# Attention and quantized FFN block on eight cores: the sign additions of the weight preparation move ahead of the next tile's scaling on VectorE

## The chip, the cores and the metric

One Trainium2 chip, all 8 NeuronCores. Every core runs the same program on its own data. The metric is the device time in microseconds (us) of the slowest core; lower is better.

## What is computed

Each of 4 sequences has 4096 tokens of width 1024; a core computes the output of one half of a sequence (2048 tokens, 16 tiles of 128), but needs keys and values of all 32 tiles.

```python
q = softmax((x @ Wq.T + bq) @ Wfq.T + bfq)      # x is layer-normed; k likewise with Wk, Wfk
v = x @ Wv.T + bv
scores = einsum('bhsd,bhtd->bhst', q, k)        # 16 heads of 64
ctx = einsum('bhst,bhtd->bhsd', scores / scores.sum(-1), v)
x = x + ctx
# FFN on layernorm(x); every matrix product is "bitlinear":
scale = 1 / mean(abs(w));   wq = clip(round(w * scale), -1, 1) / scale      # weights: -1, 0, +1
scale = 127 / max(abs(x));  xq = clip(round(x * scale), -128, 127) / scale  # activations, per token
x = x + bitlinear(silu(bitlinear(h, w_gate)) * bitlinear(h, w_up), w_down)
```

Since no exponent stands between scores and values, the kernel keeps one matrix (k times v, summed over all tokens) instead of scores.

## The kernel before, in words

The program is written as five lists of instructions, one for each engine, in the order in which the Python code emits them (class `Plan`). The order on an engine is the order of emission; between engines there are semaphores: `dv`, `ac` and `pe` emit for VectorE (DVE), ScalarE (ACT) and TensorE (PE), and each wait names a counter (`cDV`, `cAC`, `cPE`) and the value it must have reached. No scheduler moves anything.

The stages follow one another: the attention weights are combined (to 264 us), the sweep over the 32 token tiles (264 to 1326 us), then the gate and up weights are loaded and the first two FFN products run for 16 tiles (`main_mm`), then the down product. The loads for the FFN stage wait for a fence on all counters at the sweep's end.

The sweep is the loop `for t in range(TKV)` at L588. For a tile t it does:

- L597 (DVE): `xr_buf` = the tile times its reciprocal deviation, from the statistics that the turn before made.
- L604 (PE): eight transposes of `xr_buf` into `pbtr`; L610 (DVE) copies `pbtr` to `xrT`.
- L541 to L552 (PE, in `emit_proj`): the key projection into `pbA`, then the value projection into `pbV`, 16 + 4 matmuls each. L616 (DVE) takes the row maximum, L619 (ACT) the exponent, L627 and L632 (DVE) write the scaled values to `vstage`, L650 (PE) adds k times v into `pbK`.
- `emit_next_tile_stats`: the load of tile t + 1 (issued on SyncE, SP, L573) and its statistics (L329 to L348 on DVE, L352 and L356 on ACT, L360 to L371). For t < 16 the query projection and its exponent and transposes follow (L660 to L679).

Beside that runs the preparation of the three FFN weights, 24 chunks of 128 x 4096 numbers. Tiles 0 to 11 carry the first pass, sums of absolute values (`emit_prep1`, L404). At tile 12 `emit_finalize` makes the three thresholds. Then the second pass: at the end of each of the turns 13 to 24, two chunks get their signs on ACT (`emit_prep2_signs`, L492 and L497: two passes over the chunk, one with the threshold added, one with it subtracted), and the loads of two further chunks are issued from ACT's queue (L479). The sum of the two sign images is the quantized chunk: `emit_prep2_add`, L510 on DVE, which waits for L497 (`cAC`), and the store L516 on SP, which waits for L510. `prep2_drain_adds` emits all additions whose signs have been emitted; before the change it is called at L600, in the turn that follows, between L597 and the transposes of that turn. So the turns 14 to 25 hold two additions each.

SP's list around a turn is: two stores of chunks (L516), then the load of the tile after next (L573).

Of the kernel before, what the change touches and what calls it, by code (L numbers as in the profile page):

```python
# [76 lines left out]
def build_nc(TQ=16, TKV=32, dbg=()):  # L77
# [395 lines left out]
    def emit_prep2_load(k):  # L473
        wi, wdram, sl_, dst_ = prep_chunks[k]
        s = k % 2
        lsem = ("dWP", "dWP1")[s]
        prep2_ld[k] = dma("scalar", lsem,
                          lambda e, wdram=wdram, sl_=sl_, dst_=dst_, s=s:
                          e.dma_start(dst_(pchunk, s), sl_(wdram.ap())),  # L479
                          waits=[("cAC", prep2_ac.get(k - 2)),  # L480
                                 ("cAC", prep1_ac[len(prep_chunks) - 2 + s])])
# [21 lines left out]
    def emit_prep2_add(k):  # L503
        wi, wdram, sl_, dst_ = prep_chunks[k]
        sdram = (s_q["g"], s_q["u"], s_q["d"])[wi]
        s = k % 2
        ssem = ("dWS", "dWS1")[s]
        SGP = ppb[:, s * 4 * D:(s + 1) * 4 * D]
        PWQ = pwq[:, s * 4 * D:(s + 1) * 4 * D]
        vW = dv(lambda e, SGP=SGP, PWQ=PWQ: e.tensor_tensor(  # L510
            PWQ, SGP, PWQ, op=ALU.add),
            waits=[("cAC", prep2_ac[k])], drain=True)
        prep2_dv[k] = vW
        prep2_st[k] = dma("sync", ssem,
                          lambda e, sdram=sdram, sl_=sl_, dst_=dst_, s=s:
                          e.dma_start(sl_(sdram.ap()), dst_(pwq, s)),  # L516
                          waits=[("cDV", vW)])

    def prep2_drain_adds():
        while p2a[0] < p2s[0]:  # L520
            emit_prep2_add(p2a[0])
            p2a[0] += 1
# [65 lines left out]
    for t in range(TKV):  # L588
# [8 lines left out]
        xr_dv[t] = dv(lambda e, xap=xap, t=t, XR=XR: e.tensor_single_scalar(  # L597
            XR, xap, stat[:, STT["r"] + t:STT["r"] + t + 1], op=ALU.mult),
            waits=[(xw_sem, vL), ("cAC", stats_marks[t][1])])
        prep2_drain_adds()  # L600

        vT = None
        for j in range(CH):
# [91 lines left out]
        if fin_done[0]:  # L695
            for _ in range(2):
                if p2l[0] < NP2 and p2l[0] - p2s[0] < 2:
                    emit_prep2_load(p2l[0])
                    p2l[0] += 1

    while prep_i < len(prep_chunks):
        emit_prep1(prep_i)
# [541 lines left out]
```

How the kernel before makes its waits and increments, by code:

```python
                    def body(e):  # L63
                        for fn, waits, inc, inc_by, drain in stream:
                            for sem, val in waits:
                                e.wait_ge(sems[sem], val)
                            if drain:
                                e.drain()
                            inst = fn(e)
                            if inc is not None:
                                inst.then_inc(sems[inc], inc_by)
```

## Time and profile before

| | us |
|---|---|
| median of 2 runs | 2328.51 |
| the two runs | 2325.71, 2331.30 |
| the profiled execution | 2329.61 |
| its span, slowest core (7) | 2328.0 |
| spans of the eight cores | 2305.4 to 2328.0 |
| outside the span | 1.6 |

The profile below is of core 7 unless a group says otherwise. Starts are us from the first instruction; "idle before" is how long the engine had stood still, with what ended it behind the arrow. The granted clock of TensorE is given as a share of 2.4 GHz: 0.5 is the lower of its two levels, 1.2 GHz.

### The profile page before, as it was taken

How to read it: one execution, taken by the hardware profiler on the slowest of the kernel's cores; microseconds unless marked ns; L12 is line 12 of the kernel's file. 1: busy time of each engine (PE TensorE's matmuls, PEld its weight loads, DVE VectorE, ACT ScalarE, POOL GpSimd, SP SyncE). 2: the span in 40 equal slices, each digit the busy share in tenths (PEclk: the TensorE clock that was granted, in tenths of full speed). 3: DMA queues.
4: the chain of work that ended last, by engine and by line, in shares of the span. 5: the costliest groups of instructions: out<-in, count | busy, mean ns of one | idle time of the engine just before them, and what ended most of it. 6: DMA issues, size and time to landing. Idle time of an engine off the chain costs nothing.

```text
span 2328.0 us, 17906 instructions; the slowest of 8 cores (2305.4 to 2328.0 us)
## 1 busy us (share of the span) xinstructions
PE 1425.0 (61%) x5961; PEld 569.4 (24%) x5961; DVE 701.6 (30%) x1363; ACT 681.8 (29%) x641; POOL 10.1 (0%) x19
## 2 busy tenths in 40 slices
PE   0154676677774624343356516888787878528999
PEld 0021222222222211111112102333333333203444
DVE  0011322322323333332333313545454545200111
ACT  0000032233223353534410012565555555300000
POOL 0000000000000000000000000000000000000000
PEclk9987877666566766565667657999989999758999
DMA  8631044334434546455410194212121221375554
GB/s 118 96 60 36 13 159 172 130 127 171 143 115 137 193 147 209 155 197 195 157 65 26 46 199 103 82 42 81 48 76 51 72 59 50 67 133 135 145 147 133
DMA packets 309130, 261.32 MB, mean 112 GB/s; under 512 B 262640, under 2 KB 262768, under 8 KB 305776
## 3 DMA queue, kind: packets, MB, share of 16 engines
q10 hardware_dynamic: 144384, 132.13, 19.9%
q1 hardware_dynamic: 160160, 117.55, 16.0%
q0 software_dynamic: 4496, 10.50, 3.4%
q8 instruction: 49, 0.80, 0.1%
q14 instruction: 41, 0.34, 0.0%
HBM read 159.50 MB, written 69.21 MB: 98 GB/s over the span
## 4 chain that ended last, share of the span: by engine, by line
PE 37%; DMA 24%; ACTq 10%; DVE 9%; ACT 9%; issue 5%; SPq 3%; DVEq 2%; POOLq 0%
ACTq L68 9%; PE pbA L1005 7%; PE pbV L1014 6%; PE pbA L541 6%; DMA xt_buf<-x_oth 6%; PE pbV L1160 5%; PE pbA L1160 5%; DMA pchunk<-wg 3%; DMA pchunk<-wu 3%; DMA pchunk<-wd 3%; DMA wdT<-s_dq 3%; PE pbA L250 3%; DMA wfqT<-s_wfq 3%; ACT tq L1056 2%; ACT hqb L1060 2%
## 5 line engine op out<-in xcount | busy, mean ns | idle before, releaser
L1005 PE MATMUL pbA<-wgT,aq2T 128*128 128x512 bf16 x1024 | 272.0, 413 | 124.4 <-ACT silu_b L1020 55.1
L541 PE MATMUL pbA<-wckT,xrT 128*128 128x512 bf16 x512 | 201.0, 563 | 199.5 <-DVE xrT L610 199.5
L1014 PE MATMUL pbV<-wuT,aq2T 128*128 128x512 bf16 x1024 | 252.5, 390 | 36.6 <-DMA wuT<-s_uq 36.6
L1028 DVE SCALAR_TENSOR_TENSOR hmid<-pbV,smal,silu_b 128x512 f32<-128x512 f32 x128 | 96.0, 750 | 319.1 <-ACT silu_b L1020 203.7
L1160 PE MATMUL pbA<-wdT,hqT 128*128 128x512 bf16 x512 | 125.8, 397 | 75.8 <-DMA wdT<-s_dq 75.8
L1005 PEld LDWEIGHTS pbA<-wgT,aq2T 128*128 128x128 bf16 x1024 | 102.9, 103 | 267.3 <-issue 169.0
L1014 PEld LDWEIGHTS pbV<-wuT,aq2T 128*128 128x128 bf16 x1024 | 103.3, 101 | 171.3 <-issue 60.0
L541 PEld LDWEIGHTS pbA<-wckT,xrT 128*128 128x128 bf16 x512 | 60.3, 128 | 320.0 <-issue 308.7
L404 ACT ACTIVATE pp<-pchunk 128x4096 f32<-128x4096 f32 x24 | 86.8, 3617 | 167.5 <-DMA pchunk<-wg 59.7
L541 PE MATMUL pbV<-wvT,xrT 128*128 128x512 bf16 x512 | 133.4, 407 | 0.0
L1020 ACT ACTIVATE silu_b<-pbA,smal 128x512 f32<-128x512 f32 x128 | 88.0, 687 | 127.7 <-PE pbA L1005 86.8
L541 PE MATMUL pbA<-wcqT,xrT 128*128 128x512 bf16 x256 | 91.7, 522 | 52.2 <-DVE rzkb L624 35.4
L616 DVE TENSOR_REDUCE nmax<-pbA 128x1 f32<-128x1024 f32 x32 | 39.2, 1225 | 253.1 <-PE pbA L552 253.1
L1160 PE MATMUL pbV<-wdT,hqT 128*128 128x512 bf16 x512 | 111.8, 379 | 0.0
L619 ACT ACTIVATE ek_buf<-pbA,nmax 128x1024 bf16<-128x1024 f32 x32 | 35.4, 1107 | 257.3 <-DVE nmax L616 257.3
L250 PE MATMUL pbA<-wfqT,wq_nat 128*128 128x512 bf16 x128 | 31.3, 401 | 116.4 <-DMA wfqT<-s_wfq 106.0
L510 DVE TENSOR_TENSOR pwq<-ppb,pwq 128x4096 bf16<-128x4096 bf16 x24 | 55.0, 2292 | 130.2 <-ACT pwq L497 130.2
L1056 ACT ACTIVATE tq<-hmid,smal 128x1024 f16<-128x1024 f32 x64 | 73.5, 1148 | 63.7 <-DVE smal L1048 59.8
L1034 DVE TENSOR_REDUCE hmx<-hmid 128x1 f32<-128x512 f32 x128 | 87.8, 686 | 11.7
L492 ACT ACTIVATE ppb<-pchunk,bcast 128x4096 bf16<-128x4096 f32 x24 | 89.0, 3709 | 2.0
L497 ACT ACTIVATE pwq<-pchunk,bcast 128x4096 bf16<-128x4096 f32 x24 | 89.0, 3708 | 2.0
L1160 PEld LDWEIGHTS pbA<-wdT,hqT 128*128 128x128 bf16 x512 | 50.8, 99 | 149.6 <-issue 94.5
(135 smaller groups left out, 1239.6 us busy)
## 6 DMA issues: line engine op xcount, KB each, us to landing
pchunk<-wg ACTq DMA_DIRECT2D x16, 2048.0 KB, 12.2
pchunk<-wu ACTq DMA_DIRECT2D x16, 2048.0 KB, 12.4
pchunk<-wd ACTq DMA_DIRECT2D x16, 2048.0 KB, 10.5
xt_buf<-x_own SPq DMA_DIRECT2D x32, 512.0 KB, 5.5
s_hq<-hqb SPq DMA_DIRECT2D x16, 1024.0 KB, 6.6
s_gq<-pwq SPq DMA_DIRECT2D x8, 1024.0 KB, 9.1
xt_buf<-x_oth SPq DMA_DIRECT2D x16, 512.0 KB, 14.0
s_uq<-pwq SPq DMA_DIRECT2D x8, 1024.0 KB, 9.5
```

What stands on the lines that cost most here:

```text
L68: e.drain()
L250: e.matmul(pbA[:, 512 * h:512 * h + 512], w_nat[:, cj * D + mi * 128: cj * D + mi * 128 + 128], wfT[:, cj * D + 512 * h: cj * D + 512 * h ...
L492: ac(lambda e, s=s, thn=thn, SGP=SGP: e.activation(SGP, pchunk[:, s * 4 * D:(s + 1) * 4 * D], ACTF.Sign, bias=bcast[:, GLO[thn]:GLO[thn] + ...
L497: vSM = ac(lambda e, s=s, nthn=nthn, PWQ=PWQ: e.activation(PWQ, pchunk[:, s * 4 * D:(s + 1) * 4 * D], ACTF.Sign, bias=bcast[:, GLO[nthn]:G ...
L541: vlast = pe(lambda e, h=h, c=c, pb=pb, XRT=XRT, wT=wT: e.matmul(pb[:, 512 * h:512 * h + 512], XRT[:, c * 128:(c + 1) * 128], wT[:, c * D ...
L1005: vG = pe(lambda e, c=c, oc=oc, gp=gp, s=s: e.matmul(gp[:, 0:512], aq2T[:, s * D + c * 128:s * D + (c + 1) * 128], wgT[:, c * DI + 512 * o ...
L1014: vU = pe(lambda e, c=c, oc=oc, up_=up_, s=s: e.matmul(up_[:, 0:512], aq2T[:, s * D + c * 128:s * D + (c + 1) * 128], wuT[:, c * DI + 512 ...
L1020: vSI = ac(lambda e, ss=ss, gp=gp, sm=sm: e.activation(silu_b[:, ss * 512:(ss + 1) * 512], gp[:, 0:512], ACTF.Silu, bias=0.0, scale=smal[: ...
L1028: e.scalar_tensor_tensor(hmid[:, oc * 512:(oc + 1) * 512], up_[:, 0:512], smal[:, sm + 6:sm + 7], silu_b[:, ss * 512:(ss + 1) * 512], op0= ...
L1034: dv(lambda e, oc=oc, s=s: e.reduce_max(hmx[:, s * 8 + oc:s * 8 + oc + 1], hmid[:, oc * 512:(oc + 1) * 512], axis=AX, apply_absolute_value ...
L1056: vTQh = ac(lambda e, sl_=sl_, s=s, sm=sm: e.activation(tq16[:, s * D:(s + 1) * D], hmid[:, sl_ * D:(sl_ + 1) * D], ACTF.Copy, bias=1536.0 ...
L1160: e.matmul(pb[:, 512 * jh:512 * jh + 512], HQT[:, c * 128:(c + 1) * 128], wdT[:, c * D + 512 * jh: c * D + 512 * jh + 512], start=(c == 0) ...
```

## The change

The call of `prep2_drain_adds` is taken out of its place behind L597 and put at the end of the turn, behind the signs and the loads that this turn emits. Nothing else is touched: the same instructions, buffers and transfers.

```diff
@@ -597,7 +597,6 @@
         xr_dv[t] = dv(lambda e, xap=xap, t=t, XR=XR: e.tensor_single_scalar(
             XR, xap, stat[:, STT["r"] + t:STT["r"] + t + 1], op=ALU.mult),
             waits=[(xw_sem, vL), ("cAC", stats_marks[t][1])])
-        prep2_drain_adds()
 
         vT = None
         for j in range(CH):
@@ -697,6 +696,7 @@
                 if p2l[0] < NP2 and p2l[0] - p2s[0] < 2:
                     emit_prep2_load(p2l[0])
                     p2l[0] += 1
+        prep2_drain_adds()
 
     while prep_i < len(prep_chunks):
         emit_prep1(prep_i)
```

Lines behind L600 have a number lower by one in the changed kernel (L610 is L609).

On VectorE, from the end of the statistics of a tile without query part to the projection's results, the order before was (`pwq`, `ppb` are the sign images, `xr_buf` the scaled tile, `pbtr` its transposes in PSUM, `xrT` their copy):

```order
L365 CAST negrm_bf<-stat 128x1
L371 COPY rm_row<-pbtr 1x128 [waits cPE]
L597 TENSOR_SCALAR xr_buf<-xt_buf,stat 128x1024
L510 TENSOR_TENSOR pwq<-ppb,pwq 128x4096 [waits cAC] x2
L610 COPY xrT<-pbtr 128x1024 [waits cPE]
L616 TENSOR_REDUCE nmax<-pbA 128x1 [waits cPE]
```

In the changed kernel the same place on VectorE reads:

```order
L365 CAST negrm_bf<-stat 128x1
L371 COPY rm_row<-pbtr 1x128 [waits cPE]
L510 TENSOR_TENSOR pwq<-ppb,pwq 128x4096 [waits cAC] x2
L597 TENSOR_SCALAR xr_buf<-xt_buf,stat 128x1024
L609 COPY xrT<-pbtr 128x1024 [waits cPE]
L615 TENSOR_REDUCE nmax<-pbA 128x1 [waits cPE]
```

The two additions have moved from behind the scaling to ahead of it, so the scaling stands behind their wait for ScalarE.

At the first such place, which has a query part (`eqt_st` is its transposed exponent), VectorE has before:

```order
L660 TENSOR_REDUCE nmax<-pbA 128x1
L675 COPY eqt_st<-pbtr 128x1024 [waits cPE,dS2]
L597 TENSOR_SCALAR xr_buf<-xt_buf,stat 128x1024
L510 TENSOR_TENSOR pwq<-ppb,pwq 128x4096 [waits cAC] x2
L610 COPY xrT<-pbtr 128x1024 [waits cPE]
```

and now:

```order
L659 TENSOR_REDUCE nmax<-pbA 128x1
L674 COPY eqt_st<-pbtr 128x1024 [waits cPE,dS2]
L510 TENSOR_TENSOR pwq<-ppb,pwq 128x4096 [waits cAC] x2
L597 TENSOR_SCALAR xr_buf<-xt_buf,stat 128x1024
L609 COPY xrT<-pbtr 128x1024 [waits cPE]
```

It is the same exchange, behind the query part. There are 12 such places. The lists of the other four engines, SP's with the stores and tile loads among them, keep their order.

## Rows read from the trace of the kernel before

**Rows 1.** The page's first line: spans of the cores.
```profile
span 2328.0 us, 17906 instructions; the slowest of 8 cores (2305.4 to 2328.0 us)
```

**Rows 2.** The page's 40 slices of 58.2 us: busy tenths and granted clock.
```profile
PE   0154676677774624343356516888787878528999
...
PEclk9987877666566766565667657999989999758999
```

**Rows 3.** The page's costliest groups: the addition. Busy, mean ns, idle before, releaser.
```profile
L510 DVE TENSOR_TENSOR pwq<-ppb,pwq 128x4096 bf16<-128x4096 bf16 x24 | 55.0, 2292 | 130.2 <-ACT pwq L497 130.2
```

**Rows 4.** Timeline of a turn with additions (start, length, engine, line, idle before).
```profile
1008.35 0.73 DVE L597 TENSOR_SCALAR xr_buf<-xt_buf,stat 128x1024 bf16<-128x1024 f32 x1
...
1018.58 3.71 ACT L497 ACTIVATE pwq<-pchunk,bcast 128x4096 bf16<-128x4096 f32 x1
...
1022.43 2.29 DVE L510 TENSOR_TENSOR pwq<-ppb,pwq 128x4096 bf16<-128x4096 bf16 x1 [5.28 <-ACT pwq L497]
1024.64 0.68 DVE L610 COPY xrT<-pbtr 128x1024 bf16<-128x1024 bf16 x1
1025.38 0.60 SPq L573 DMA_DIRECT2D xt_buf<-x_oth  x1
...
1032.10 1.23 DVE L616 TENSOR_REDUCE nmax<-pbA 128x1 f32<-128x1024 f32 x1 [6.77 <-PE pbA L552]
...
1036.88 1.28 DVE L627 TENSOR_SCALAR vstage<-pbV,rzkb 128x1024 bf16<-128x1024 f32 x1 [1.99 <-PE pbV L552]
...
1039.98 1.22 DVE L329 TENSOR_REDUCE stat<-xt_buf 128x1 f32<-128x1024 f32 x1 [1.72 <-DMA xt_buf<-x_oth]
```

**Rows 5.** Timeline of VectorE in a turn without additions.
```profile
1241.22 0.73 DVE L597 TENSOR_SCALAR xr_buf<-xt_buf,stat 128x1024 bf16<-128x1024 f32 x1
1243.22 0.69 DVE L610 COPY xrT<-pbtr 128x1024 bf16<-128x1024 bf16 x1 [1.26 <-PE pbtr L604]
...
1255.42 1.28 DVE L627 TENSOR_SCALAR vstage<-pbV,rzkb 128x1024 bf16<-128x1024 f32 x1 [2.00 <-PE pbV L552]
```

**Rows 6.** VectorE at L329, 737 to 1196 us, waiting for the tile load: total us, times.
```profile
  DMA xt_buf<-x_oth: 14.2, 9
```

**Rows 7.** The same for core 2.
```profile
  DMA xt_buf<-x_oth: 0.6, 1
```

**Rows 8.** Who waited for whom, 740 to 1190 us: total us, times, longest.
```profile
DVE nmax L616 <- PE pbA L552: 90.7, 12, 9.3
...
DVE vstage L627 <- PE pbV L552: 27.1, 12, 3.8
```

**Rows 9.** The same view and stretch on core 2.
```profile
DVE nmax L616 <- PE pbA L552: 106.9, 12, 9.3
...
DVE vstage L627 <- PE pbV L552: 25.2, 12, 3.7
```

**Rows 10.** Timeline of VectorE on core 2: one turn and the next one's start.
```profile
1056.80 0.69 DVE L610 COPY xrT<-pbtr 128x1024 bf16<-128x1024 bf16 x1
...
1071.36 1.28 DVE L627 TENSOR_SCALAR vstage<-pbV,rzkb 128x1024 bf16<-128x1024 f32 x1 [1.99 <-PE pbV L552]
...
1094.30 0.68 DVE L610 COPY xrT<-pbtr 128x1024 bf16<-128x1024 bf16 x1
```

**Rows 11.** Timeline of VectorE on core 0: a turn with long projections and the next.
```profile
1067.13 0.69 DVE L610 COPY xrT<-pbtr 128x1024 bf16<-128x1024 bf16 x1
...
1083.56 1.28 DVE L627 TENSOR_SCALAR vstage<-pbV,rzkb 128x1024 bf16<-128x1024 f32 x1 [3.68 <-PE pbV L552]
...
1106.51 0.68 DVE L610 COPY xrT<-pbtr 128x1024 bf16<-128x1024 bf16 x1
...
1118.84 1.28 DVE L627 TENSOR_SCALAR vstage<-pbV,rzkb 128x1024 bf16<-128x1024 f32 x1 [1.99 <-PE pbV L552]
```

**Rows 12.** Projections in two turns of core 7: PE busy, granted clock, DMA share, GB/s.
```profile
1025.40:1036.00 10.60, 10.53 (x38) 0.82 0.98 397
1098.20:1111.00 12.80, 12.77 (x29) 0.50 0.95 357
```

## The prediction

> **What bounds the kernel now.** I read the spans of the cores first: they differ by up to 22.6 us, and the profiled core 7 is the slowest [rows 1]. Of the 40 slices, those from the 14th to the 20th are the turns with additions: PE stands at 2 to 5 tenths, the granted clock at 0.5 to 0.7 [rows 2]. Nobody is saturated there; a turn is a ring of waits. The group of the addition says who sets the pace on DVE: before each of the 24 additions DVE stands idle, 130.2 us in all, and each time ACT's second sign pass ends it [rows 3]. The timeline of one turn shows the ring [rows 4]. The statistics end, ACT takes four sign passes of 3.71 us, DVE adds (2.29), copies `xrT` at 1024.64, PE projects, DVE writes `vstage` at 1036.88, and then takes the next statistics at 1039.98. The last step waits for a transfer: the tile load is issued at 1025.38, behind the two stores on SP, and ended 1.72 us of idle time. So two arms run from the last addition to the next statistics: one over `xrT` and the projections, one over the tile load. The later one closes the turn.
>
> **What the change moves.** The scaling L597 and the transposes now lie in the shade of ACT: L597 starts at 1008.35, more than 14 us before the last addition at 1022.43 [rows 4], and needs 2.00 us to the copy with the transposes between. Behind the change L597 stands behind both additions. In turns without additions `xrT` starts 1243.22 - 1241.22 = 2.00 us after L597 starts [rows 5]; L597 will start where the copy starts now. So the copy comes 2.00 us later in each of 12 turns, 24.0 us in all. The work is the same and its cover is gone. What the additions gain is nothing: in these rows L597 is over at 1009.1, and they wait for signs in any case. The stores L516 wait for the additions, which do not move, and SP's list keeps its order, so the tile load leaves as before. ACT's signs wait for statistics, as before. DVE's copy, maximum, `vstage` and statistics are queued behind the waiting instructions and all shift together.
>
> **What of the 24.0 us reaches the end.** First term: where the tile load ends last, the other arm has room. On core 7 DVE waits for it in 9 of the 12 turns, 14.2 us in all [rows 6]. A turn can cover at most 2.00 us; in three of the nine the wait is longer than that, by 1.3 us in sum, so the cover is 12.9 us. That leaves 11.1 us. On other cores the cover is smaller, down to 0.6 us on core 2 [rows 7].
>
> Second term: the granted clock. The projections take different lengths in the same turn's work. From copy to `vstage` it is 12.24 us in one turn [rows 4], 12.20 without additions [rows 5], 14.56 on core 2 [rows 10], 16.43 on core 0 [rows 11]. The difference is how late the clock rises from 1.2 to 2.4 GHz after PE has stood idle: one turn's projections ran at 0.82 of full clock, those of a long turn at 0.50 throughout [rows 12]. How much of it lies in the 12 turns can be read from what DVE waits for PE. A short turn has 6.77 + 1.99 = 8.76 us of it (6.77 ahead of L616 and 1.99 ahead of L627 [rows 4]), 105.1 us in 12 turns. Core 7 has 90.7 + 27.1 = 117.8 [rows 8], so 12.7 us come from a late clock; core 2 has 132.1 [rows 9], 27.0 us.
>
> That excess need not stay. On core 2 the copies lie 1094.30 - 1056.80 = 37.50 us apart, and the projections are 14.56 long [rows 10]; ten turns in a row repeat this. The spacing is the projections' length plus 22.94, and at about 37.5 us the next turn meets the clock as the last one did. On core 0 a long turn is followed 39.38 us later by a short one, 12.33 [rows 11]; in all eight places where the spacing was 39.3 to 39.5 the next turn was short. Behind the change the fixed part is 22.94 + 2.00 = 24.94. A turn of 14.56 then has a spacing of 39.5, which does not repeat itself; a short one of 12.3 to 12.6 has 37.2 to 37.5, which does. So I expect cores to leave the 14.56 turn and to stay mostly with short ones. On core 7 the excess of 12.7 us lies chiefly in four turns, three of them with no transfer behind; I take 10 of it as regained. The bounds are 0 (the lengths stay) and 12.7 (all short). Sum for core 7 up to the last addition: 24.0 - 12.9 - 10.0 = +1.1 us. For core 2: 24.0 - 0.6 - about 23, near zero.
>
> Third term: the six closing turns without additions and the choice of the slowest of eight. They are not changed, but their meeting with the clock is dealt again. One turn of 16.4 in place of 12.3 is 4.1 us, and the metric takes the worst of eight cores. I add 3 us, between 0 and 8. Behind the sweep everything waits on one fence, so its end passes through in full.
>
> The forecast is 2329.6 (the profiled execution, 1.1 above the median) + 1.1 + 3 = 2333.7, say 2334 us, which is +0.2%. A measurement of this kernel tells about 2% (46 us) from no change, and this is far inside.
>
> At the clock a rule of the Trainium skill can be weighed, from "TensorE: Matmul & The Clock Gate", Part 1: the array's clock is throttled by default, and sustained activity releases it. By that rule, transposes that run right ahead of the projections would count as activity and bring the rise forward; half of the 2.0 us they start earlier would be saved in each turn, some 12 us more, and the time would be about 2322. The trace does not bear it out: turns without additions have their transposes right ahead already, and are 12.20 us long against 12.24 [rows 4, 5].
>
> **Rivals.**
>
> A. *The cover and the clock both fail.* The tile load could be later by the same 2 us, or the lengths stay as they are. For it: on cores 2 and 6 nearly nothing covers the delay now. Against it: the load's issue depends on the additions alone. It gives the whole 24.0 us: 2353.6. With the cover but no clock regained it is 2329.6 + 11.1 = 2340.7, and I count that as the upper part of my forecast.
>
> B. *A colder TensorE; slower by over 2%.* The eight transposes now interrupt PE's idle time, some 14 us before the copy at 1024.64. Behind the change PE stands idle from the statistics' transpose to the late ones, and the clock could rise late in every turn. If all 12 were as the longest seen, 16.43, against the mean of core 7 of 12.24 + 12.7 / 12 = 13.3, that is 37.6 us; with the 24.0 and no cover 61.6, so 2391. It decides from a mean length of 15.3 us on (22 of 46 us). Against it: core 7's long turn [rows 12] had the transposes in the middle just like the short ones, so they do not keep the clock up. The same page of the Trainium skill, section "HAM oscillation", says that gaps in PE's work bring the clock down again; here it is down either way.
>
> C. *The clock more than pays.* All turns short and the closing turns too: -1.6 (24.0 - 12.9 - 12.7) and up to -8 in the closing turns: about 2320, where the rule of the clock page would end too. What speaks for it is the spacing above; against it, that the slowest of eight cores decides.
>
> **How the numbers follow.** Forecast, from -3 to +14 us: 0.65. A, +14 to +30: 0.17. C, below -3: 0.12. B: 0.05. Something of another size and sign: 0.01. The range takes the forecast, most of C down to 2324 (-5.6) and A down to the whole delay less a little, 2351. Faster by over 2% 0.01, slower by over 2% 0.05, within 2% 0.94.
>
> **What would show it.** In the changed trace L597 starts as the second addition ends, and L609 2.0 us later, in 12 turns: this must hold, or the first step is wrong. DVE's wait for the tile load at L329 shrinks from 14.2 us to under 5 on core 7; if it stays, the load moved and A is right. The spacing of the copies tells of the second term: about 37.4 us with lengths of 12.0 to 12.6 in most of the later turns, on core 2 above all. If the lengths stay at 14.5 with spacings of 39.5, the clock term is wrong and the time is 2341 or more; if they are 16.4 throughout, it is B. The stages ahead of 737 us and behind the fence must be the same within a few us.

## The result, and the profile after

The changed kernel takes 2337.53 us (median of 43 runs) against 2331.34 us (42 runs of the kernel before, taken beside it); the ratio is 1.0029, 95% interval 1.0015 to 1.0043. So it is slower by 6.8 us (3.5 to 10.0), within 2%. (The ratio leaves out executions in which the cores of a die ran longer at a lower clock, as happens with either kernel; the medians keep them.) The forecast was 2334, 4.1 us above the time it started from.

The page of the changed kernel, core 7: first line, the 40 slices of TensorE and its clock, and the group of the addition.

```profile
span 2333.3 us, 17907 instructions; the slowest of 8 cores (2316.9 to 2333.3 us)
...
PE   0244657676684543242446515888887878528999
...
PEclk9987876666666666666667657999989999758999
...
L510 DVE TENSOR_TENSOR pwq<-ppb,pwq 128x4096 bf16<-128x4096 bf16 x24 | 55.0, 2293 | 138.2 <-ACT pwq L497 138.2
```

Beside [rows 1 to 3] hardly anything has moved, and that is the first lesson: the page does not show this change, although 24 us of delay were put into it. VectorE's wait ahead of the additions grew from 130.2 to 138.2 us. The scaling (12 times 0.73 us) no longer fills a part of it.

The timeline of one turn of the changed kernel, core 7, answers to [rows 4]:

```profile
1032.71 2.29 DVE L510 TENSOR_TENSOR pwq<-ppb,pwq 128x4096 bf16<-128x4096 bf16 x1 [5.28 <-ACT pwq L497]
...
1034.92 0.75 DVE L597 TENSOR_SCALAR xr_buf<-xt_buf,stat 128x1024 bf16<-128x1024 f32 x1
1035.65 0.81 SPq L573 DMA_DIRECT2D xt_buf<-x_oth  x1
...
1035.81 1.01 PE L603 MATMUL pbtr<-identb,xr_buf 128*128 128x128 bf16 x8 [17.43 <-DVE xr_buf L597]
...
1036.93 0.69 DVE L609 COPY xrT<-pbtr 128x1024 bf16<-128x1024 bf16 x1 [1.26 <-PE pbtr L603]
...
1049.28 1.28 DVE L626 TENSOR_SCALAR vstage<-pbV,rzkb 128x1024 bf16<-128x1024 f32 x1 [1.99 <-PE pbV L552]
...
1050.55 1.21 DVE L329 TENSOR_REDUCE stat<-xt_buf 128x1 f32<-128x1024 f32 x1
```

The scaling starts as the second addition ends, the copy 1036.93 - 1034.92 = 2.01 us later, and L329 no longer waits for the tile load. Both steps read as forecast. In all 12 turns and on all eight cores, the distance from L597 to L609 is 2.01 or 2.02 us.

What VectorE waited for, from 740 us to 1195 us (the view of [rows 8]) and at L329 (the view of [rows 6]), on core 7:

```profile
DVE nmax L615 <- PE pbA L552: 87.4, 12, 9.3
...
DVE vstage L626 <- PE pbV L552: 23.3, 11, 3.7
...
  DMA xt_buf<-x_own: 1.5, 1
  DMA xt_buf<-x_oth: 0.3, 1
```

and on core 2 (beside [rows 9]):

```profile
DVE nmax L615 <- PE pbA L552: 85.7, 12, 8.8
...
DVE vstage L626 <- PE pbV L552: 23.5, 12, 2.0
```

On core 2 the sum fell from 132.1 to 109.2 us, on core 7 the wait for tile loads from 14.2 to 1.8. (One of core 7's twelve waits at L626 counts as ended by something else, so its sum cannot be set beside the old one.) The spacing of the copies on core 2, to set beside [rows 10]:

```profile
1095.53 0.69 DVE L609 COPY xrT<-pbtr 128x1024 bf16<-128x1024 bf16 x1 [1.27 <-PE pbtr L603]
...
1108.10 1.28 DVE L626 TENSOR_SCALAR vstage<-pbV,rzkb 128x1024 bf16<-128x1024 f32 x1 [1.99 <-PE pbV L552]
...
1133.06 0.69 DVE L609 COPY xrT<-pbtr 128x1024 bf16<-128x1024 bf16 x1 [1.27 <-PE pbtr L603]
```

The spacing is 37.53 us, as before (37.50). The fixed part is 2.0 us longer, and the projections are 12.57 us long in place of 14.56. The turn swallowed its own delay.

The granted clock says where the projections got shorter. These are the first 9.00 us from a copy to `xrT`, on core 2 of the kernel before and of the changed one (the last three numbers are granted clock, DMA share and GB/s, as in [rows 12]):

```profile
core 2: us, PE busy (x) PEld busy (x) DVE busy (x) ACT busy (x) POOL busy (x), PEclk, DMA share, GB/s
1056.80:1065.80 9.00, 7.79 (x18) 2.30 (x20) 0.69 (x2) 0.00 (x0) 0.00 (x0) 0.50 0.98 395
...
1095.53:1104.53 9.00, 7.79 (x26) 2.63 (x28) 1.90 (x2) 0.00 (x0) 0.00 (x0) 0.71 0.98 380
```

In the same 9.00 us, with the same DMA share beside it (0.98), TensorE stayed at its lower level (0.50) before and began 18 matmuls; in the changed kernel it rose to the upper level on the way (0.71 in the mean) and began 26.

For each kernel of the table I took three stretches from the starts of the copies to `xrT`: from tile 13's to tile 14's, the 12 turns with additions (tile 14's to tile 26's), and the closing turns (tile 26's copy to tile 31's `vstage`). Each is the mean of eight cores of one profiled execution. "Projections" is the sum of the 12 distances from copy to `vstage` within the second stretch; "tile load" is the sum of the waits at L329 there.

| kernel | 13 to 14 | 12 turns | projections | tile load | closing | ratio to before (95%) |
|---|---|---|---|---|---|---|
| before | 39.3 | 442.8 | 167.0 | 6.7 | 124.3 | 1 |
| changed | 41.6 | 443.4 | 151.2 | 1.3 | 126.4 | 1.0029 (1.0015 to 1.0043) |
| e1, one addition ahead (7 cores) | 39.4 | 444.5 | 169.1 | 6.2 | 125.7 | 0.9983 (0.9966 to 0.9999) |
| e2, delay 2.2, nothing moved | 41.5 | 444.4 | 150.6 | 1.2 | 114.5 | 0.9959 (0.9933 to 0.9986) |
| e3, delay 1.1, nothing moved | 40.4 | 445.6 | 160.3 | 3.6 | 128.3 | 1.0020 (1.0003 to 1.0037) |
| e4, changed, 1.1 more | 42.7 | 469.7 | 166.3 | 0.3 | 130.7 | 1.0116 (1.0088 to 1.0145) |
| e5, before, early tile load | 39.3 | 437.8 | 169.2 | 0 | 124.5 | 0.9958 (0.9929 to 0.9988) |
| e9, changed, early tile load | 41.6 | 442.2 | 151.5 | 0 | 129.9 | 1.0006 (0.9989 to 1.0023) |
| e6, changed, one push of 1.6 | 41.0 | 444.4 | 150.6 | 1.2 | 129.6 | 1.0037 (1.0005 to 1.0068) |

The 12 turns hold 11 of the delays: 22.0 us. Of these, 5.4 went into the wait for tile loads (6.7 to 1.3) and 15.8 into shorter projections (167.0 to 151.2), which leaves 0.8; measured is 0.6. Ahead of them lie 2.3 us, the first delay, and behind them 2.1 in the closing turns. That makes 5.0 us for the mean core up to the end of the sweep. (Behind the sweep the mean core took 999.0 us before and 1003.7 in the changed kernel, for the same instructions; the other profiled kernels of the table lie between 998.5 and 1001.9 there. Over all executions of the ratio the mean core's span grew by 5.3 us, from 2319.8 to 2325.1, which is the sweep's 5.0 and leaves next to nothing for the stages behind it.)

The 12 turns show one number again and again. Where a core settled, the spacing is about 37.54 us whatever the fixed part: 22.94 + 14.60 before, 24.95 + 12.58 in the changed kernel, 25.15 + 12.39 in e2. The projections take what is left.

### The profile page after: what moved, and what is told of

Read it like the earlier page. It is cut to its first block, busy times and chain, and to the rows that moved or that the text cites. A ratio compares the mean times of both kernels' runs of the same rounds, so it can differ in the third digit from the quotient of the medians.

```text
span 2333.3 us, 17907 instructions; the slowest of 8 cores (2316.9 to 2333.3 us)
## 1 busy us (share of the span) xinstructions
PE 1417.3 (61%) x5961; PEld 568.9 (24%) x5961; DVE 702.0 (30%) x1363; ACT 681.8 (29%) x641; POOL 10.1 (0%) x19
## 4 chain that ended last, share of the span: by engine, by line
PE 40%; DMA 20%; DVE 10%; ACTq 10%; ACT 9%; issue 5%; SPq 3%; DVEq 2%; POOLq 0%
ACTq L68 9%; PE pbA L541 8%; PE pbA L1005 7%; PE pbV L1014 6%; PE pbV L1160 5%; PE pbA L1160 5%; DMA pchunk<-wg 4%; DMA pchunk<-wu 3%; PE pbV L541 3%; DMA pchunk<-wd 3%; DMA wdT<-s_dq 3%; PE pbA L250 3%; DMA wfqT<-s_wfq 3%; ACT tq L1056 2%; ACT hqb L1060 2%
## 5 line engine op out<-in xcount | busy, mean ns | idle before, releaser
L603 PE MATMUL pbtr<-identb,xr_buf 128*128 128x128 bf16 x256 | 32.4, 307 | 237.6 <-DVE xr_buf L597 237.6
L541 PE MATMUL pbV<-wvT,xrT 128*128 128x512 bf16 x512 | 128.4, 396 | 0.0
L618 ACT ACTIVATE ek_buf<-pbA,nmax 128x1024 bf16<-128x1024 f32 x32 | 35.4, 1108 | 276.1 <-DVE nmax L615 276.1
L510 DVE TENSOR_TENSOR pwq<-ppb,pwq 128x4096 bf16<-128x4096 bf16 x24 | 55.0, 2293 | 138.2 <-ACT pwq L497 138.2
## 6 DMA issues: line engine op xcount, KB each, us to landing
pchunk<-wg ACTq DMA_DIRECT2D x16, 2048.0 KB, 12.2
```

The costliest lines, as they stand in the source:

```text
L541: vlast = pe(lambda e, h=h, c=c, pb=pb, XRT=XRT, wT=wT: e.matmul(pb[:, 512 * h:512 * h + 512], XRT[:, c * 128:(c + 1) * 128], wT[:, c * D ...
```

## The experiments

### e1: one of the two additions ahead of the scaling

```diff
+        if p2a[0] < p2s[0]:
+            emit_prep2_add(p2a[0])
+            p2a[0] += 1
         xr_dv[t] = dv(lambda e, xap=xap, t=t, XR=XR: e.tensor_single_scalar(
...
         prep2_drain_adds()
```

> The kernel before, with only the first of the two additions moved ahead of the scaling L597; the second stays behind it. Theory (the cost is the 2.00 us of scaling and transposes that lost their cover behind the LAST addition's wait): L597 now sits between the two additions, still covered by the wait for the second chunk's signs, so the copy to xrT follows the second addition at once and the time is that of before, within 3 us. Rival (any addition ahead of the scaling costs, by the order as such): half of the change, +3 us, or, if the first addition is what counts, all of it.

VectorE of e1, the slowest core (L613 is the copy):

```profile
1021.58 2.29 DVE L510 TENSOR_TENSOR pwq<-ppb,pwq 128x4096 bf16<-128x4096 bf16 x1 [6.44 <-ACT pwq L497]
1023.79 0.75 DVE L600 TENSOR_SCALAR xr_buf<-xt_buf,stat 128x1024 bf16<-128x1024 f32 x1
1029.15 2.29 DVE L510 TENSOR_TENSOR pwq<-ppb,pwq 128x4096 bf16<-128x4096 bf16 x1 [4.62 <-ACT pwq L497]
1031.36 0.68 DVE L613 COPY xrT<-pbtr 128x1024 bf16<-128x1024 bf16 x1
```

2331.93 us against 2335.42, ratio 0.9983. The scaling sits between the additions, the copy follows the second at once, and the 12 turns and their projections are near those of before (444.5 and 169.1 us against 442.8 and 167.0). No loss shows in the time, so the rival is out; it is even 3.5 us lower, a little outside the 3 us expected. What costs is the work behind the last wait, not the order as such. (On one core a record of VectorE is missing; the table leaves that core out.)

### e2 and e3: the delay without the move

Operations that rewrite a scratch tile with its own values stand behind the additions, two in e2 and one in e3. They are 1.01 us long, and 1.10 apart.

```diff
         prep2_drain_adds()
+        if 14 <= t < 26:
+            dv(lambda e: e.scalar_tensor_tensor(
+                sq_scr[:, 0:820], sq_scr[:, 0:820], 1.0, sq_scr[:, 0:820],
+                op0=ALU.mult, op1=ALU.max), drain=True)
```

> The kernel before, additions in their old place, with two idle operations of about 1.0 us each on VectorE behind the second addition in turns 14 to 25 (they rewrite a scratch tile with its own values). It delays the copy to xrT by 2.0 us as the change does, but leaves scaling and transposes early. Theory (only the delay of 2.0 us counts): as the changed kernel, +4 to +8 us over before, spacings of the copies locked at 37.5 us with projections of 12.5. Rival (the place of the transposes matters for TensorE's clock): the projections stay at 14.5 and the time is +15 to +24 us.

e2, VectorE of core 0 (L618 is the copy, L635 `vstage`):

```profile
1017.61 1.01 DVE L602 SCALAR_TENSOR_TENSOR sq_scr<-sq_scr 128x820 f32<-128x820 f32 x1
1018.71 1.01 DVE L606 SCALAR_TENSOR_TENSOR sq_scr<-sq_scr 128x820 f32<-128x820 f32 x1
1019.64 0.68 DVE L618 COPY xrT<-pbtr 128x1024 bf16<-128x1024 bf16 x1
1032.03 1.28 DVE L635 TENSOR_SCALAR vstage<-pbV,rzkb 128x1024 bf16<-128x1024 f32 x1 [2.00 <-PE pbV L552]
...
1057.19 0.68 DVE L618 COPY xrT<-pbtr 128x1024 bf16<-128x1024 bf16 x1
```

The turns behave as in the changed kernel: spacing 1057.19 - 1019.64 = 37.55, projections 12.39, 150.6 us in 12 turns. The transposes' place plays no part that shows, since here they run early. But the time missed the expectation: it is not 4 to 8 us over before but 2323.92 against 2335.42, ratio 0.9959 (0.9933 to 0.9986), with 2.2 us of idle work added to every turn. The table says where most of it lies: in the closing turns, which nobody touched, 114.5 to 114.6 us on all eight cores in place of 119.8 to 125.7. That is what e6 was made for.

> The same with one operation, a delay of 1.0 us in each of 12 turns. Theory (the spacing of the turns sets how late TensorE's clock rises): the sum is 12 us, less some 7 us of cover by the tile load on a core like core 7, less what the clock gives back; by the lengths read at each spacing, +1 to +6 us over before. Rival (each us of delay beyond the cover costs its length, the clock is luck): cores 2 and 4 with no cover show +12 us and the slowest core +8 to +12.

e3, VectorE of core 2 (L614 is the copy, L631 `vstage`):

```profile
974.94 0.68 DVE L614 COPY xrT<-pbtr 128x1024 bf16<-128x1024 bf16 x1
987.39 1.28 DVE L631 TENSOR_SCALAR vstage<-pbV,rzkb 128x1024 bf16<-128x1024 f32 x1 [2.00 <-PE pbV L552]
...
1011.44 0.68 DVE L614 COPY xrT<-pbtr 128x1024 bf16<-128x1024 bf16 x1
1026.00 1.28 DVE L631 TENSOR_SCALAR vstage<-pbV,rzkb 128x1024 bf16<-128x1024 f32 x1 [2.00 <-PE pbV L552]
...
1050.05 0.68 DVE L614 COPY xrT<-pbtr 128x1024 bf16<-128x1024 bf16 x1
```

2337.86 us, ratio 1.0020 (1.0003 to 1.0037), which is 4.7 us slower. Here no single length repeats: 12.45 and 14.56 take turns, with spacings of 36.50 and 38.61, together 75.11, twice 37.55. The mean of the 12 turns is 2.8 us longer for 12.1 us of added work, and the time lies within the theory's +1 to +6. Of the two cores that the rival named, core 2 refutes it (442.9 us against 443.5) and core 4 does not: 451.4 against 440.6, near the rival's 12. Core 4 entered the 12 turns another way than before (42.3 us from tile 13 to 14 in place of 39.0), waited 9.9 us for tile loads in place of 0.7, and had two turns of 16.4 and 16.6 us in a row. On the other six cores the change is between -0.8 and +7.0 us.

### e4: one microsecond more on top of the change

```diff
+        if 14 <= t < 26:
+            dv(lambda e: e.scalar_tensor_tensor(
+                sq_scr[:, 0:820], sq_scr[:, 0:820], 1.0, sq_scr[:, 0:820],
+                op0=ALU.mult, op1=ALU.max), drain=True)
         xr_dv[t] = dv(lambda e, xap=xap, t=t, XR=XR: e.tensor_single_scalar(
```

> The changed kernel with one more idle operation of 1.0 us behind the second addition in the same 12 turns, a delay of 3.0 us against before. Theory (spacing and clock): the spacing can no longer settle at 37.5 us with short projections (12.55 + 25.95 = 38.5); lengths of 14 and 16 us come back, so the added 12 us of operations cost 18 to 30 us over the changed kernel. Rival (no coupling): +12 us over the changed kernel, with its short projections kept.

e4, VectorE of core 2 (L613 is the copy, L630 `vstage`):

```profile
1001.37 0.69 DVE L613 COPY xrT<-pbtr 128x1024 bf16<-128x1024 bf16 x1 [1.26 <-PE pbtr L607]
1017.98 1.28 DVE L630 TENSOR_SCALAR vstage<-pbV,rzkb 128x1024 bf16<-128x1024 f32 x1 [3.85 <-PE pbV L552]
...
1044.04 0.69 DVE L613 COPY xrT<-pbtr 128x1024 bf16<-128x1024 bf16 x1 [1.27 <-PE pbtr L607]
1056.62 1.28 DVE L630 TENSOR_SCALAR vstage<-pbV,rzkb 128x1024 bf16<-128x1024 f32 x1 [2.00 <-PE pbV L552]
...
1082.68 0.69 DVE L613 COPY xrT<-pbtr 128x1024 bf16<-128x1024 bf16 x1 [1.26 <-PE pbtr L607]
```

2363.25 us (four executions), ratio 1.0116 (1.0088 to 1.0145). The 12 turns grew by 26.3 us over the changed kernel for 12 us of added work, inside the theory's 18 to 30 and far from the rival's 12. No single turn repeats, but three in a row do: lengths of 16.61, 12.58 and 12.1, with spacings of 42.67, 38.64 and about 38.1. Most of the turns are short ones; the third with 16.6 is what makes the stretch long. So the cost of a delay in these turns is no line. Against before, delays of 1.1, 2.0, 2.2 and 3.1 us in each turn make the 12 turns longer by 2.8, 0.6, 1.6 and 26.9 us.

### e5 and e9: without the tile load's arm

In both the load of the next tile is issued on SyncE ahead of the stores of the chunks. e5 does it to the kernel before, e9 to the changed one, so their difference is the change with nothing to cover it. The edit of e5 is shown; e9 puts the load ahead of the additions at the turn's end, where the changed kernel has them.

```diff
             waits=[(xw_sem, vL), ("cAC", stats_marks[t][1])])
+        if t + 1 < TKV:
+            emit_xload(t + 1)
         prep2_drain_adds()
```

> The kernel before, with the load of the next tile issued on SyncE ahead of the two stores, at the turn's start. It takes the second arm away: the tile is there long before the statistics. Theory: VectorE's 14.2 us of waiting for tile loads on core 7 (11 us on cores 0, 3, 5) goes to about 0, but what those turns give back is taken by the clock, since without the transfer the spacing settles at 37.5 us with projections of 14.6: stretch of the 12 turns with additions unchanged within 3 us, time within 5 us of before. Rival (the loads bound these turns): the slowest core gains the whole wait, 11 to 14 us.

> The changed kernel with the tile load issued ahead of the stores. The tile load's arm, which covered part of the delay, is gone on every core; against the same edit of the kernel before (e5) nothing is left to cover the 2.0 us in 12 turns. Theory (the clock takes back most of it by the spacing): projections settle at 12.5 us, spacing 37.5, the stretch of the 12 turns 440 to 443 us, that is 0 to +6 us over that of e5 (435.8 to 442.9), and the time 2328 to 2338. Rival (cover alone made the change cheap): +24 us over e5 in the stretch, some 460 us, and 2349.

The waits at L329 are gone in both.

e5 takes 2324.81 us against 2331.5, ratio 0.9958 (0.9929 to 0.9988), which is 9.8 us faster (2.8 to 16.5). That missed my expectation of 5 us, and the interval holds the rival's 11 to 14. The stretch of the 12 turns shows the same: of 6.7 us of waiting for tile loads on the mean core 5.0 came out as time, and the projections grew by only 2.2 us. Six cores fell into a cycle with lengths near 16.4, 12.4 and 11.8 (435.8 to 436.9 us for the 12 turns), two into the 14.5 of before (442.8 and 442.9). So the clock did not take back what the early load gave.

e9 takes 2332.93 us, ratio 1.0006. Its 12 turns are 442.2 us, 4.4 over e5, where 22.0 us of delay lie uncovered; the projections fell from 169.2 to 151.5. The rival's 24 us in this stretch are refuted: most of the delay is regained there with no transfer to hide behind. But 4.4 is not the whole price. The first delay adds 2.3 us and the closing turns 5.4 (124.5 to 129.9), so e9 lies 12.2 us over e5 at the end of the sweep, half of the 24, where the changed kernel lies 5.0 over before. The spans of all executions that the ratios use say the same: against the kernel before, the mean of the eight cores is 14.4 us shorter in e5 (2305.4 against 2319.8) and 0.3 longer in e9 (2319.1 against 2318.8). Inside the 12 turns the clock is the larger part of why the change is cheap; over the whole sweep the cover by the tile load counts as well.

### e6: one push ahead of the closing turns

```diff
+        if t == 26:
+            for _ in range(2):
+                dv(lambda e: e.scalar_tensor_tensor(
+                    sq_scr[:, 0:600], sq_scr[:, 0:600], 1.0, sq_scr[:, 0:600],
+                    op0=ALU.mult, op1=ALU.max), drain=True)
         xr_dv[t] = dv(lambda e, xap=xap, t=t, XR=XR: e.tensor_single_scalar(
```

> The changed kernel with idle work of about 1.6 us on VectorE, ONCE, ahead of the scaling of tile 26, the first of the six closing turns. Theory (how the closing turns meet the clock is decided by when the additions end): cores whose closing stretch is the long one (133 us from the copy of tile 26 to vstage of tile 31, as cores 0, 2 and 5 of the changed kernel) get shorter by 6 to 10 us although work was added, those with the short one (120 us) get longer by 5 to 8; the slowest core gains 3 to 6 us. Rival (the closing turns do not depend on it): every core 1.6 us later.

In the changed kernel a core whose turn of tile 25 has projections of 14.2 us takes 133.1 us for its closing turns, one with 12.6 takes 120.1. In e6 it is the other way round: 120.1 on the two cores with 14.2, and 132.9 to 133.0 on the four with 12.5 to 12.6 (the last two, with 11.8, take 132.3; the one such core of the changed kernel 131.7). Core 2 stands for both, with projections of 14.23 us in tile 25 in either kernel. Its closing stretch, in the changed kernel and then in e6:

```profile
1193.45:1326.58 133.13, 90.91 (x319) 30.80 (x325) 40.15 (x84) 9.26 (x22) 0.00 (x0) 0.67 0.08 28
...
1193.27:1313.39 120.12, 77.60 (x319) 28.70 (x325) 40.15 (x83) 9.26 (x22) 0.00 (x0) 0.73 0.09 31
```

The 13.0 us are TensorE's: its busy time falls from 90.91 to 77.60 us for the same 319 matmuls, VectorE's (40.15) and ScalarE's (9.26) stay, and the granted clock is 0.73 in place of 0.67. Nothing but 1.6 us of idle work, once, lies between. The direction is as expected and the size larger, 13 us in place of 6 to 10 and 5 to 8. The expected gain of the slowest core did not come: 2342.71 us, ratio 1.0037 (1.0005 to 1.0068), about what the changed kernel has. In the profiled execution only two of the eight cores were of the kind that it helps, and the slowest was not one of them. One gets a throw of the dice, not a gain.

### e7, e8 and e10: the opposite move

If work behind the last wait is what costs, everything that needs no sign should go ahead of it.

```diff
@@ e7: L600 goes, the call stands behind L616
-        prep2_drain_adds()
...
             nmax[:, s:s + 1], pbA[...], axis=AX, negate=True),
             waits=[("cPE", vK)])
+        prep2_drain_adds()
@@ e8: e7, and the tile load ahead of it
+        if t + 1 < TKV:
+            emit_xload(t + 1)
@@ e10: e8, and each chunk load right behind the signs that free its buffer
                 emit_prep2_signs(p2s[0])
                 p2s[0] += 1
+                if p2l[0] < NP2:
+                    emit_prep2_load(p2l[0])
+                    p2l[0] += 1
```

> The opposite move: the additions are put behind the row maximum L616 of the same turn, so scaling, transposes, copy and projections all run beneath ScalarE's sign passes. Tile load still behind the stores on SyncE. Theory (two arms): the arm over the projections, some 16 us, gets out of the way, and the tile load's arm, which leaves with the second addition and lands about 14.5 us after it, becomes the bound: 15.2 + 2.3 + 14.5 + 5.4 = 37.4 us minus what a less loaded DMA gives back, so a turn of 33 to 37 us and a time 0 to 40 us below before. Rival (the projections alone bound the turn): spacing of about 25 us, 140 us faster.

e7, the slowest core: the two additions (joined in one line) to the next statistics.

```profile
949.15 4.68 DVE L510 TENSOR_TENSOR pwq<-ppb,pwq 128x4096 bf16<-128x4096 bf16 x2
...
954.32 1.28 DVE L627 TENSOR_SCALAR vstage<-pbV,rzkb 128x1024 bf16<-128x1024 f32 x1 [0.41 <-PE pbV L552]
954.48 0.42 SPq L573 DMA_DIRECT2D xt_buf<-x_oth  x1
...
969.14 1.22 DVE L329 TENSOR_REDUCE stat<-xt_buf 128x1 f32<-128x1024 f32 x1 [13.45 <-DMA xt_buf<-x_oth]
```

2332.57 us, ratio 0.9996 (0.9964 to 1.0028). The projections are off the path, and the time is the same: the tile load's arm took over whole, as the first theory has it at its upper end. The waits at L329 are 152.6 us for the mean core, and the 12 turns 451.2. (The additions now come behind the copy, so this stretch holds 12 pairs of them in place of 11. From tile 13's copy to tile 26's, which holds all 12 in every kernel, it is 477.1 us against 482.1 before.)

> The same with the tile load issued ahead of the stores, so both arms are taken away. Theory: the turn is ScalarE's 15.2 us of signs, the additions or the exponent behind them, vstage and the statistics, some 24 us, unless the 4 MB of chunk loads in a turn, issued behind the signs and landing in 12 to 15 us, hold it at 27 to 31; so 70 to 150 us faster than before (2180 to 2260). Rival (something else holds the turns near 37 us): as e7.

e8, the slowest core, one turn:

```profile
941.84 3.71 ACT L492 ACTIVATE ppb<-pchunk,bcast 128x4096 bf16<-128x4096 f32 x1
...
944.78 1.22 DVE L617 TENSOR_REDUCE nmax<-pbA 128x1 f32<-128x1024 f32 x1 [9.27 <-PE pbA L552]
945.62 3.71 ACT L497 ACTIVATE pwq<-pchunk,bcast 128x4096 bf16<-128x4096 f32 x1
...
949.48 2.29 DVE L510 TENSOR_TENSOR pwq<-ppb,pwq 128x4096 bf16<-128x4096 bf16 x1 [1.09 <-ACT pwq L497]
949.90 1.11 ACT L621 ACTIVATE ek_buf<-pbA,nmax 128x1024 bf16<-128x1024 f32 x1 [0.57 <-ACT pwq L497]
...
953.21 1.21 DVE L329 TENSOR_REDUCE stat<-xt_buf 128x1 f32<-128x1024 f32 x1
```

2183.86 us (four executions), ratio 0.9348 (0.9302 to 0.9394): 148 us faster than before, with both arms gone. The row maximum is done while ScalarE is still at its signs, the exponent starts 0.57 us behind the last of them, and L329 waits for nothing. A turn takes 302.2 / 12 = 25.2 us in place of 36.9, and from tile 13's copy to tile 26's it is 327.9 us in place of 482.1. (The distance from copy to `vstage`, 189.0 us in 12 turns, is no length of the projections any more: in this turn `vstage` follows the second addition and the exponent at 951.94 and waits for no matmul.)

> e8 with each chunk load issued right behind the signs of the chunk whose buffer it takes, in place of both behind the second one: the loads leave 7.6 us apart. Theory: in e8's turns (25 us) no sign pass waits for a chunk load; ScalarE waits for a store of 1 MB still reading the sign image (2.64 us in one turn). Spreading the loads evens the transfers, so the same time as e8 or up to 15 us less. Rival: the loads collide with the stores, 5 to 10 us more.

2172.91 us (four executions), ratio 0.9313 (0.9292 to 0.9334). By the medians this is 11 us below e8, but the two intervals overlap; the 12 turns take 298.0 us in place of 302.2 in one execution of each. So the rival's loss of 5 to 10 us does not show, and a gain over e8 is not shown. It is the lowest time of the study, 6.9% below before.

## Why the prediction was right

In short: the delay came as forecast, the tile load covered a part of it, and shorter projections gave most of the rest back inside the 12 turns. That the forecast's 4.1 us and the measured 6.8 (3.5 to 10.0) lie so near each other is in part luck, because on core 7, for which the sum was made, the terms for the clock and for the closing turns came out 5 and 9 us off, in opposite directions, and its longer span arose ahead of the change.

*The copy comes 2.00 us later in each of 12 turns.* Shown by the timeline (2.01 us) and by e1, which moves an addition and keeps the cover.

*The tile load covers 12.9 us on core 7.* On that core its wait fell by 12.4 us (14.2 to 1.8). For the mean core it is 5.4, and e9 against e5 shows that the change costs 4.4 us in the 12 turns where nothing is covered at all. The term was right for core 7. Over the whole sweep e9 lies 12.2 us over e5, so the cover is needed, if less than one for one.

*The clock gives back 10 us on core 7 and some 23 on core 2, because the turn settles at 37.5 us with short projections.* The place and the mechanism were right: the lengths went to 12.5 at spacings of 37.4 to 37.5 in the later turns of every core, the granted clock shows the earlier rise, and e2 shows that it is the delay, and not the moved work, that does it. e3 and e4 show how the spacing decides: with 1.1 us the turns alternate, with 3.1 us every third is long again. The size on the named core was off. Core 7's projections fell by 5.1 us (159.8 to 154.7), because two of its turns, those of tiles 15 and 16, came out at 16.4 and 14.5 us ahead of the settling. Up to the last addition it lost 5.8 us (482.3 to 488.1 from tile 13's copy to tile 26's), not 1.1. The rule of the spacing had an exception in the trace of before that the prediction does not name: on cores 2 and 6 a spacing of 39.5 behind tile 15, a turn with a query part, was followed by 14.5 and not by a short turn. On core 2 it was 22.8 us (174.2 to 151.4), as written.

*3 us for the closing turns and the slowest of eight, between 0 and 8.* The mean core lost 2.1 us there. But core 7 gained 5.6 us (125.7 to 120.1). So from tile 13's copy to the end of the sweep it took 608.0 us before and 608.2 in the changed kernel: its own sum is near zero, and its span is 5.3 us longer because it reached tile 13's copy 5.5 us later (714.2, 719.8), ahead of all changed turns. The mean core reached it 1.1 us earlier, so this is no effect of the change that these runs show. The bounds for the closing turns were too small: single cores show closing stretches of 114.5 (e2), 120.1 (changed), 125.7 (before), 133.1 (changed) and 136.1 us (e4) for the same instructions, a spread of 21.6.

Two small readings: in [rows 2] the 14th slice has TensorE at 6 tenths, and only those from the 15th to the 20th are low, at 2 to 4. In rival B the limit of 22 us over 12 turns is a mean length of 15.1 us, not 15.3.

The rivals: A, the full 24 us, would need the clock not to answer and no cover. Neither held. B, a colder TensorE, is refuted for this delay by the fallen projections. e4 shows lengths of 16.6 returning in every third turn with one microsecond more; its transposes are as late as the changed kernel's, so their place is not what brings them. C was too hopeful by the closing turns, though e2 shows that such an outcome exists. The rule of the Trainium skill that was weighed ("TensorE: Matmul & The Clock Gate", Part 1) says that activity releases the clock. That transposes count as such activity was a step of the prediction, and the runs give it no support: the changed kernel with late transposes has 151.2 us of projections in its 12 turns, e2 with early ones and nearly the same delay 150.6, where the rule so read would have made the changed kernel's shorter by some 12 us.

What stays open: why six cores of e5 fell into one cycle and two into another, and why core 4 of e3 did not settle, was not followed up. Each profile is one execution, and the deal differs between executions. Nor do the runs give a rule that foretells the closing stretch from the turns ahead of it; that it depends on when the additions end is shown (e6), which end gives which stretch was only sorted by the length of tile 25.

## What to carry to other kernels

Work that needs nothing from a wait should stand ahead of it on its engine, and the question to ask of a moved wait is what now stands behind it, on every arm that leaves from the same instruction. Here the additions' place decided between 2338 us (ahead of the scaling), 2331 (behind it) and, once the tile load was freed too, 2173 (behind the projections, chunk loads spread). One arm alone gave nothing (e7) or 0.4% (e5), both together 6.5% (e8). In a loop in which TensorE idles every turn, price a small delay by the spacing of the turns as well: read the spacing and the length of the matmul stretch in several turns and cores before calling a term hidden or lost.

## What the runs showed of the hardware that was not expected

The time is not monotone in the work. Idle work of 2.2 us in each of 12 turns made the kernel 0.4% faster (e2), 3.1 us of delay made it 1.2% slower (e4), and 1.6 us of idle work once turned a closing stretch of 133.1 us into 120.1, and one of 120.1 into 133.0 (e6). In all of them the same matmuls ran; what differed was the clock granted to them, 0.67 of full speed over the closing stretch of 133.1 us and 0.73 over that of 120.1. I had expected this coupling inside the turns with additions, from the repeating lengths in the trace of before, but not that it would shift a stretch of six untouched turns by up to 21.6 us (114.5 in e2, 136.1 on six cores of e4), more than the whole change costs. Where the turns settle, the spacing stays at 37.5 us under fixed parts of 22.94, 24.95 and 25.15, and in e3, with a fixed part of 24.05 between them, two turns together take twice that. So a delay of 1 or 2 us in such a loop can cost next to nothing, and the one of 3.1 us costs 26.9 in 12 turns.
